# A recurrent layer's input stage pipelined over three engines, and layer norms begun inside the experts stages before them

## What is computed

```python
# layer 0: feed-forward of 8 experts, all computed, each token's output scaled and masked
h = silu(xf @ gw.T) * (xf @ uw.T);  out = out + mask[:, None] * (h @ dw.T) * mean_w
# layer 2, recurrent part
xz = x @ in_proj_w.T + in_proj_b;  x_main, z = split(xz)        # 256 columns each
xc = silu(causal_conv(x_main, 4 taps) + conv_b)
ssm = xc @ x_proj_w.T + x_proj_b                                # B, C and delta's column
delta = softplus(ssm[..., -1:]);  A = -exp(A_log)
h_t = exp(A * dt_t) * h_(t-1) + dt_t * B_t * x_t;  y_t = h_t . C_t + D * x_t
y = (y * silu(z)) @ out_proj_w.T + out_proj_b                   # then norm(y + residual)
# layer 3 attention: a norm of the normed input, with gamma and beta, then q, k, v
```

## Time and profile before

| | us |
|---|---|
| median of 3 runs | 2511.35 (2510.97 to 2511.7) |
| profiled execution | 2498.77 |
| its span, first to last instruction | 2497.0 |
| mean granted TensorE clock in it | 0.887 of full |

### The profile page before, as it was taken

One profiled execution on the slowest core, in us unless ns is written; L12 is line 12 of the kernel. 1 busy time (PEld: TensorE's weight loads), 2 busy tenths in 40 slices (PEclk: granted clock), 3 DMA queues, 4 the chain that ended last, 5 costly groups with the idle time before them and its releaser, 6 DMA issues. The chain is left out here.

```text
span 2497.0 us, 36481 instructions
## 1 busy us (share of the span) xinstructions
PE 2065.9 (83%) x12192; PEld 1383.8 (55%) x12216; DVE 1664.6 (67%) x4206; ACT 1048.7 (42%) x2330; POOL 552.1 (22%) x909
## 2 busy tenths in 40 slices
PE   7697999987998797557775898499499979999888
PEld 3354788874555455223332455388234438777777
DVE  5576677776765575559998465455688956666655
ACT  2354222222664453255552344422257744444433
POOL 0342111102110430138884421010211010000010
PEclk8698899996997799679997699699679989999989
DMA  8320000004110420000001420000321110000000
GB/s 332 97 60 21 1 1 1 1 1 127 52 43 20 116 60 1 1 0 1 0 1 56 105 47 21 1 1 1 130 67 48 38 43 1 1 1 1 1 1 18
DMA packets 60073, 94.75 MB, mean 38 GB/s; under 512 B 11312, under 2 KB 33136, under 8 KB 58736
## 3 DMA queue, kind: packets, MB, share of 16 engines
q1 hardware_dynamic: 29792, 55.57, 6.6%
q0 software_dynamic: 29952, 36.45, 6.0%
q10 hardware_dynamic: 144, 0.39, 0.1%
HBM read 65.63 MB, written 31.29 MB: 39 GB/s over the span
## 5 line engine op out<-in xcount | busy, mean ns | idle before, releaser
L986 DVE TENSOR_REDUCE m<-banks 128x1 f32<-128x512 f32 (+3 forms) x512 | 272.5, 584 | 90.4 <-PE banks L1150 49.3
L2635 PEld LDWEIGHTS banks<-w_ffn,eh 128*128 128x128 f32 x2144 | 280.1, 191 | 21.2
L2635 PE MATMUL banks<-w_ffn,eh 128*128 128x128 f32 x2144 | 281.7, 275 | 0.0
L1118 ACT ACTIVATE p<-banks 128x512 f32<-128x512 f32 (+3 forms) x512 | 233.7, 522 | 93.2 <-PE banks L1196 54.2
L1421 DVE TENSOR_REDUCE m<-banks 128x2 f32<-128x308 f32 x384 | 165.8, 475 | 148.8 <-PE banks L1713 80.9
L2623 PE MATMUL banks<-x_hi,w_hi 128*128 128x512 f32 x472 | 210.7, 446 | 17.4 <-PEq L332 17.4
L1148 PE MATMUL banks<-K,Qf 32*128 32x512 f32 (+2 forms) x512 | 179.4, 501 | 16.3 <-PEq L332 11.2
L2625 PE MATMUL banks<-x_hi,w_lo 128*128 128x512 f32 x472 | 188.1, 399 | 0.0
L2624 PE MATMUL banks<-x_lo,w_hi 128*128 128x512 f32 x472 | 188.1, 398 | 0.0
L2605 ACT ACTIVATE et<-banks 128x512 f32<-128x512 f32 x140 | 83.7, 598 | 244.8 <-PE banks L2625 244.8
L3019 PE MATMUL banks<-hc,w_start 128*128 128x512 f32 x256 | 126.2, 615 | 45.6 <-POOL hc L2955 45.6
(11 more groups left out here) (424 smaller groups left out, 4358.9 us busy)
## 6 DMA issues: line engine op xcount, KB each, us to landing
Qf<-stack_q_plain POOLq DMA_DIRECT2D x48, 256.0 KB, 3.0
Qf<-stack_q_masked POOLq DMA_DIRECT2D x32, 256.0 KB, 3.0
K<-stack_k_self POOLq DMA_DIRECT2D x32, 256.0 KB, 3.1
w_ffn<-ffn_dram SPq DMA_DIRECT2D x1, 6144.0 KB, 35.3
stack_q_plain<-q_hi SPq DMA_DIRECT2D x24, 256.0 KB, 3.0
stack_q_masked<-q_hi SPq DMA_DIRECT2D x16, 256.0 KB, 3.0
stack_k_self<-k_hi SPq DMA_DIRECT2D x16, 256.0 KB, 3.6
K<-stack_k_ctx POOLq DMA_DIRECT2D x48, 80.0 KB, 2.7
```

The costliest lines, as they stand in the source:

```text
L986: ins = dve.reduce_max(k.m[:, t, h:h + 1], bank[:, 0:(t + 1) * P if k.kind == "page" else S], AX)
L1118: nc.scalar.activation(k.p[:, x % PBUFS, q0:S], score_banks[x % 3][:, q0:S], ACT.Exp).then_inc(sem("exp_done"), 1)
L2635: last = pe.matmul(bank[:, t * P:(t + 1) * P], k.h[:, n % RING, t * P:(t + 1) * P], w(down.format(e))[:, i * P:(i + 1) * P], start=(i == 0 ...
```

## The change

Six things change. (1) In `scan_inputs` PE projects two batches ahead, c has three buffers, z and zt two, ACT's order of first taps, tanh and gate is another, and the gate is one DVE instruction in place of two on POOL; diag has four buffers; one of the three parts of B and C is copied by POOL instead of ACT. (2) `scan_prepare` is gone: its instructions stand in `scan_inputs`, in waits. (3) `experts_block` can norm the first `ahead` batches for the stage behind it, in pieces between its steps; for this the last two experts run batch by batch. It is asked for three batches before "a1", two before the recurrent layer, and two double norms before "a3". (4) `narrow_project` norms what is left batch by batch, and (5) in "a3" gamma and beta become scale and bias of the ACT instruction that copies the transposed tile. (6) In `cross_block` POOL starts unit 2's load before batch 2's and 3's low queries, and the mask rows are stored by ACT's queue, after batch 0's queries are taken.

```diff
@@ cross_block, gpsimd
                 load_stacks(n)
-            for b in range(1, B):
+            low_queries(1)
+            load_stacks(2)
+            for b in range(2, B):
                 low_queries(b)
             for n in range(LAST):
                 values(n)
-                if n + 2 < LAST:
+                if n >= 1 and n + 2 < LAST:
                     load_stacks(n + 2)
@@ cross_block, scalar
             take_queries(0)
+            if k.masked:
+                store_mask_rows()
             for b in range(1, B):
                 take_keys(b)
@@ experts_block
-    pairs = [(e, b) for e in range(experts) for b in range(B)]
+    apart = experts - min(experts, 2) if ahead else experts
+    pairs = [(e, b) for e in range(apart) for b in range(B)]
+    pairs += [(e, b) for b in range(B) for e in range(apart, experts)]
+    pieces = DOUBLE_PIECES if norm_kind == "double" else PIECES
+    stretch = (experts - apart) * tiles
+    begin = apart * B * tiles + stretch + 2
...
                 if i == 1 and m >= 1:
                     add_expert(m - 1)
+                b, piece = divmod(n - begin, max(stretch, pieces))
+                if 0 <= b < ahead and piece < pieces:
+                    norm_piece(b, piece)
+            done = max(0, len(work) - begin)
+            for b in range(ahead):
+                for piece in range(pieces):
+                    if b * max(stretch, pieces) + piece >= done:
+                        norm_piece(b, piece)
             add_expert(len(pairs) - 1)
@@ narrow_project, vector
-            norm(0)
-            norm(1)
-            if page:
-                rotate(0)
-            norm(2)
-            if page:
-                for b in range(1, B):
+            lead = early + 1 if early else 2
+            for b in range(early, lead):
+                norm(b)
+            for b in range(B):
+                if page:
                     rotate(b)
+                if lead + b < B:
+                    norm(lead + b)
@@ scan_inputs
+            def gate(b):
+                dve.wait_ge(sem("tanh_z"), b + 1)
+                dve.scalar_tensor_tensor(k.zs[:, b], zt[:, b % 2], 1.0, z[:, b % 2], ALU.add, ALU.mult).then_inc(sem("zs_ready"), 1)
...
                 activate(b)
+                gate(b)
+            for i in range(2):
+                last = dve.tensor_scalar(k.D[:, i, :], w("ident"), w("m_d")[:, i:i + 1], None, ALU.mult)
+            ch.link(last)
...
+            pool.wait_ge(sem("part_ready"), 2)
             for b in range(B):
...
+                last = nc.gpsimd.tensor_copy(k.bc[32:64, b * S:(b + 1) * S], parts[32 * b:32 * b + 32, 1])
...
             project(0)
+            project(1)
             for b in range(B):
-                if b + 1 < B:
-                    project(b + 1)
+                if b + 2 < B:
+                    project(b + 2)
                 parameters(b)
```

More of the change, by code:

```diff
@@ L431, in __init__ @@
         self.bits = sb("bits", [P, tiles], I32)
+        self.first = sb("first", [P, tiles])
         if tiles == QT:
@@ L678, in vector_rsqrt, with vector_newton @@
     ch.link(dve.tensor_scalar(n.rstd[:, at].bitcast(I32), n.bits[:, at], -1.0, float(0x5F3759DF), ALU.mult, ALU.add))
-    for _ in range(3):
+def vector_newton(dve, ch, n, at, steps):
+    for _ in range(steps):
         ch.link(dve.tensor_tensor(n.sq[:, at], n.rstd[:, at], n.rstd[:, at], ALU.mult))
@@ L810, in take_x @@
                 act.wait_ge(sem("xT_done"), b + 1)
-                nc.scalar.copy(xnT[:, b * S:(b + 1) * S], ps[6 + b % 2][:]).then_inc(sem("xnT_ready"), 1)
+                at, bank = xnT[:, b * S:(b + 1) * S], ps[6 + b % 2][:]
+                if page:
+                    taken = nc.scalar.copy(at, bank)
+                else:
+                    taken = nc.scalar.activation(at, bank, ACT.Identity, scale=w("a3_g"), bias=w("a3_b"))
+                taken.then_inc(sem("xnT_ready"), 1)
             def take_latent(b):
@@ L2571, in add_expert, with norm_piece @@
                 last.then_inc(sem("x_added"), 1)
+            def norm_piece(b, i):
+                if i == 0:
+                    dve.wait_ge(sem("x_added"), pairs.index((experts - 1, b)) + 1)
+                if norm_kind == "double":
+                    vector_double_piece(dve, ch, net, b * QT, (b + 1) * QT, i)
+                else:
+                    vector_norm_piece(dve, ch, net.x, net.n, b * QT, (b + 1) * QT, i)
             for n, (m, i) in enumerate(work):
@@ L2643, in _ @@
                     output(n - 2)
+    net.normed = ahead
     end_of_block(net)
-NSTATE, NCONV = 16, 4
+NSTATE, NCONV, CONVS = 16, 4, 3
 OWN = 384
@@ L2848, in _ @@
                 for t in range(QT):
-                    last = pe.matmul(ps[b][:, t * P:(t + 1) * P], w("ones"), diag[:, b % 2, t, :], start=(t == 0), stop=True, skip_group_check=True)
+                    last = pe.matmul(ps[b][:, t * P:(t + 1) * P], w("ones"), diag[:, b, t, :], start=(t == 0), stop=True, skip_group_check=True)
                 last.then_inc(sem("spread_done"), 1)
-    end_of_block(net)
-def scan_prepare(net, k):
-    nc, sem, w = net.nc, net.sem, net.w
-    with nc.Block() as block:
-        @block.scalar
-        def _(act):
-            nc.scalar.activation(k.A[:], w("m_alog"), ACT.Exp).then_inc(sem("A_exp"), 1)
-        @block.vector
-        def _(dve):
-            ch = Chain(dve, sem("dve_chain"))
-            for i in range(2):
-                last = dve.tensor_scalar(k.D[:, i, :], w("ident"), w("m_d")[:, i:i + 1], None, ALU.mult)
-            ch.link(last)
-            dve.wait_ge(sem("A_exp"), 1)
-            ch.link(dve.tensor_scalar(k.A[:], k.A[:], -1.0, None, ALU.mult))
     end_of_block(net)
@@ L3121, in program, with experts @@
             pass
-        def experts(weight, route, act_kind, names, n, tiles, keep_x=False):
+        def experts(weight, route, act_kind, names, n, tiles, keep_x=False, norm_kind=None, ahead=0):
             stack, sb = scope()
@@ L3131, in experts @@
                     route(net, r)
-                experts_block(net, e, act_kind, names, n, tiles)
+                experts_block(net, e, act_kind, names, n, tiles, norm_kind, ahead)
         stack, sb = scope()
@@ L3157, in program @@
         wait_loaded("ffn0")
-        experts("f0_router", route_mean, "silu", ("w{}", "d{}"), E8, 4)
+        experts("f0_router", route_mean, "silu", ("w{}", "d{}"), E8, 4, norm_kind="one", ahead=3)
         ffn0_room.close()
@@ L3171, in program @@
         end_of_block(net)
-        experts(None, None, "silu", ("L1_w", "L1_d"), 1, 3)
+        experts(None, None, "silu", ("L1_w", "L1_d"), 1, 3, norm_kind="one", ahead=2)
         ffn1_room.close()
@@ L3198, in program @@
         wait_loaded("ffn2")
-        experts("f2_router", route_sinkhorn, "relu", ("w{}", "d{}"), E8, 2, keep_x=True)
+        experts("f2_router", route_sinkhorn, "relu", ("w{}", "d{}"), E8, 2, keep_x=True, norm_kind="double", ahead=2)
         ffn2_room.close()
```

153 lines of the change are left out of this document (82 added, 71 removed).

## The result

The changed kernel takes 2434.82 us (median of 4 executions, 2432.13 to 2440.75), the kernel before on the same chip 2511.16 us (4 executions): a ratio of 0.9702, 95% interval 0.9682 to 0.9722, so 76 us less. On another chip it was 2434.08 us beside 2500.46: 0.9723 (0.9689 to 0.9758), 66 us less. The forecast was 2444 us, 67 us less, with a range of 2430 to 2461. Time and sign stand in the range.

What follows compares the result with a forecast made beforehand. With TensorE 83% busy, only its idle time or the chain ahead of it was taken to count. Terms summed to -66.8 us, taking 2511.35 to 2444 us; range 2430 to 2461 (8 in 10).

Steps and rivals of the forecast that it cites:

- scan_prepare: Stage before the scan: its work moves under waits, one barrier stays, table load precedes first dA; -1.8 us (0 to -3.1).
- a1: Paged projection: three norms done beforehand, so TensorE loses most waits and slow matmuls; -16.5 us (-13 to -19).
- a3: Last projection: only two batches' norms remain, plus GpSimd's low parts and one batch's way through; -19 us (-13 to -22).
- Scan inputs, front: Recurrent layer's input stage, up to raw: gate contention and the chain through TensorE go; -31 us (-23 to -34).
- Rival A: Lower clock and contention eat a third, TensorE at 1.2 GHz through scan inputs: 2461 us; chance 0.25 shared with another rival.
- Tail: End of scan inputs: four new GpSimd copies contend with VectorE's short two-input instructions; +2 us.
- Experts: Experts stages that take on norms for later stages: eight-expert silu +2 us, one-expert silu +5.5, relu +7.7.
- Cross: First two cross stages: earlier third Qf load removes TensorE's waits, mask rows leave SyncE's queue; -11.5 us (-8 to -15).
- From profile to median: Whole kernel: the timed median's 12.6 us above the profiled execution was carried over to the forecast.

Runs made afterwards that it cites:

- short_tail: Changed kernel with B and C's second part copied by ScalarE, Exp table loaded right after the logarithm, one-expert stage norming one batch, not two: 2428.34 us (0.9708).

## Why the prediction was right, point by point

- **Scan inputs, front**: -31.1 for -31. The schedule held: I had the last xc done 26.9 us after the first tap, it was 27.9, and raw 5.1 us later instead of 3.3, because PE is still at the third batch's parameters then. The choice in this term was that PE keeps the upper level; a granted 0.84, 1.00, 0.68 and 1.00 in the four groups, against 0.50, bear it out in the main. (Rival A's "0.50 for every parameters group" was misread: the last group before, 1085.3 to 1089.1, has 1.00 and takes 3.8 us.) What I had not seen is that the two causes do not add (the gate's move brings 7.0 alone and 15.2 as the second).
- **Tail**: +2.0 for +2, by luck: contention, the whole of my term, made 1.1, and the other 0.9 is the spread, which took 6.61 us at a granted 0.56 instead of 5.70 at 0.68 and which I had put at 0. **scan_prepare**: -2.6 for -1.8; the table load cost 0.6 us of its 1.28, since before the first dA had been ready some 0.7 us ahead of the scan. The merge was not tried by itself.
- **a1**: -17.2 for -16.5, and **a3**: -18.8 for -19. In "a3" the six low parts hold norm steps for 5.7 us where I counted 4.5.
- **Experts**: +6.6 for +7.7 and +4.6 for +5.5, both 1 us too high. In the relu experts all nine pieces of the norm, 8.0 us, stand ahead of the last addition, not eight of 8.4; from the last matmul to the barrier that is 7.3 us more, and the stage up to there is 0.7 shorter. In the one-expert stage my own terms, 1.4 + 5 - 1.25, give 5.15 and not the 5.5 written; measured are 1.0 + 4.9 - 1.25. The eight-expert stage took 295.2 to 298.3 us in ten executions with its norms and 295.3 to 297.1 in four without them, so its term, +2, measures 0.7 by the means, which a scatter of 3 us does not tell from 0.
- **Cross**: -11.2 for -11.5, all of it by the load, since the kernel with the late load has nothing left of it. The 11.5 holds 5.0 + 5.2 for the waits, 0.5 for the mask rows, which is not shown, and 0.8 for the clock without a working. The second stage gained 6.7 us where its wait was 5.2.
- **From profile to median**: here 7 of the 9 us arose; the other 2 are the terms above, whose errors of about 1 us or less have both signs and partly cancel. I carried 12.6 us over from before to after as if they belonged to the kernel. Single executions do not bear that: spans differ by 12.2 us between two of the kernel before, by 4.1 between two of after, and the profiled execution of after was 5.9 us above its median, not below it. On the first chip the medians differ by 76, on the second by 66, and the touched stages by 69 and 71. The kernel before took 2508 to 2512 us on the first chip and had medians of 2500 to 2502 on three others, after 2434.8 and 2434.1 on two; what makes that difference is open.

## What to carry to other kernels

An order and a contention that act on the same chain are not to be priced apart and added. Chains of tiny VectorE steps cost by the step and not by the width (0.17 us for 4 columns and for 12), so merge batches before you distribute the chain over other stages, and price the pieces that end up behind the last matmul in full.

## What the runs showed of the hardware

- An attention stage with unchanged instructions took from 200.4 to 215.2 us over executions, at granted clocks from 0.86 to 0.75. A difference of 10 us between two single profiles of this kernel proves nothing; that of a stage whose own code changed does, where it is clear of what the stage varies by itself (3 us in the eight-expert stage, 2.3 in the first cross stage of the kernel before).
- GpSimd's copy of 32x512 in bfloat16 takes 0.8 us (3.17 for four), and beside it a 128x16 VectorE step takes up to 0.61 us instead of 0.17.
- A stage that hands over a faster TensorE can lose the gain in the next: 1.5 us won and 1.4 lost over one barrier, and the same again in `short_tail`.
